# The last pipelined step of a patch-sum, attention and mixture-of-experts kernel gets an instruction order of its own

## What is computed

```python
pooled = x.reshape(B, 12, 14, 16, 14, 16).sum(axis=(3, 5))      # sums over 16x16 patches
h = einsum('bcij,ce->bije', pooled, channel_weights)            # tokens
h = h + attn(layernorm(h))      # 12 heads of 16; weights relu(1 + qk + qk^2/2), normalised by their sum
# mixture of 8 experts, the top 2 of a softmax over the router's logits
flat = layernorm(h); top_w, top_i = top_k(softmax(flat @ router_w.T), 2)
for e in range(8):
    out = out + w_e * (gelu(flat @ w1[e] + b1[e]) @ w2[e] + b2[e])
h = h + out
```

## Time and profile before

| | us |
|---|---|
| median of 3 executions | 1339.64 |
| lowest and highest | 1336.73, 1343.89 |
| the profiled execution, its own time | 1337.59 |
| its span in the trace | 1335.8 |
| PE busy in the span | 1217.7 (91%) |
| DVE, ACT, POOL busy | 903.1, 608.4, 589.5 |
| mean granted TensorE clock | 0.945 |

### The profile page before, as it was taken

How to read it: one execution, slowest core, us unless ns; L and a number is a source line. 1 busy time by engine, 2 the same in 40 slices (tenths; PEclk the granted TensorE clock), 3 DMA queues, 4 the chain that set the end, 5 groups by cost and what they waited for, 6 DMA issues and landing times.

```text
span 1335.8 us, 26425 instructions
## 1 busy us (share of the span) xinstructions
PE 1217.7 (91%) x7299; PEld 1086.3 (81%) x7299; DVE 903.1 (68%) x3022; ACT 608.4 (46%) x1159; POOL 589.5 (44%) x484
## 2 busy tenths in 40 slices
PE   5867766999999989999999999999999989999996
PEld 3756655888888878888888888888888879898996
DVE  6789887787878677878777687878764323332443
ACT  1222223454545444545454455555454534444664
POOL 0104334415545445454535545454545465433433
PEclk9986566999999999999999999999999989999998
DMA  9679887777978787878787978888735565544565
GB/s 357 231 263 333 326 279 254 237 223 242 243 243 238 231 220 239 245 242 236 245 228 226 242 239 233 249 237 250 193 99 106 170 142 109 102 96 92 118 144 113
DMA packets 126551, 284.41 MB, mean 213 GB/s; under 512 B 24820, under 2 KB 70501, under 8 KB 126501
## 3 DMA queue, kind: packets, MB, share of 16 engines
q1 hardware_dynamic: 82762, 241.95, 54.9%
q0 software_dynamic: 43104, 41.25, 18.3%
q10 hardware_dynamic: 634, 0.61, 0.2%
HBM read 228.79 MB, written 54.95 MB: 212 GB/s over the span
## 4 chain that ended last, share of the span: by engine, by line
PE 40%; DVE 17%; DMA 16%; issue 13%; POOL 11%; ACT 2%; POOLq 0%; ACTq 0%; DVEq 0%; SPq 0%
PE ps L998 13%; PE ps L967 12%; DMA result<-ys,ridx 8%; POOL rows_d L610 7%; DMA rows_d<-rows,sloti 7%; DVE red L1074 6%; POOL result L625 4%; PE ps L807 3%; PE ps L938 3%; PE ps L939 3%; DVE topi L1208 1%; DMA w1r<-L_attn_w_qkv 1%; DVE att L1192 1%; PE ps L1027 1%; PE ps L893 1%
## 5 line engine op out<-in xcount | busy, mean ns | idle before, releaser
L625 POOL DMA_INDIRECT result<-ys,ridx x210 | 329.9, 1571 | 311.0 <-issue 142.0
L998 PE MATMUL ps<-w2a,hid 128*128 x2520 | 455.6, 327 | 0.0
L998 PEld LDWEIGHTS ps<-w2a,hid 128*128 128x128 f32 x2520 | 415.8, 191 | 11.8 <-issue 0.2
L610 POOL DMA_INDIRECT rows_d<-rows,sloti x256 | 251.1, 981 | 382.8 <-DMA rows_d<-rows,sloti 158.3
L1074 DVE TENSOR_REDUCE red<-xbuf 128x21 f32<-128x672 f32 x448 | 359.0, 842 | 5.1 <-PE ps L871 2.4
L732 ACT ACTIVATE hid<-ps,b1s 128x512 f32<-128x512 f32 (+1 forms) x344 | 222.7, 654 | 235.5 <-PE ps L967 226.3
L967 PE MATMUL ps<-xh,w1h 128*128 128x512 f32 (+1 forms) x344 | 164.8, 479 | 8.9 <-DVE xl L1302 5.3
L1325 DVE TENSOR_TENSOR w1l<-w1r,w1h 128x768 fp32r<-128x768 f32 x116 | 110.4, 953 | 76.4 <-ACT w1h L744 75.7
L967 PE MATMUL ps<-xh,w1l 128*128 128x512 f32 (+1 forms) x344 | 130.5, 379 | 0.0
L967 PE MATMUL ps<-xl,w1h 128*128 128x512 f32 (+1 forms) x344 | 130.5, 379 | 0.0
L967 PE MATMUL ps<-xb,w1l 128*128 128x512 f32 (+1 forms) x344 | 130.3, 379 | 0.0
(11 more groups left out here) (160 smaller groups left out, 1569.7 us busy)
## 6 DMA issues: line engine op xcount, KB each, us to landing
xbuf<-x SPq DMA_DIRECT2D x224, 672.0 KB, 5.7
w1r<-L_ffn_w SPq DMA_DIRECT2D x118, 384.0 KB, 4.5
xr<-rows_d SPq DMA_DIRECT2D x48, 402.0 KB, 3.5
result<-h1s SPq DMA_DIRECT2D x32, 294.0 KB
w2a<-L_ffn_w SPq DMA_DIRECT2D x8, 576.0 KB, 7.8
rows_d<-rows,sloti POOLq DMA_INDIRECT x256
rows_d<-pad SPq DMA_DIRECT2D x9, 402.0 KB, 4.4
result<-ys,ridx POOLq DMA_INDIRECT x210
```

Of the source, the lines that this page charges most:

```text
L610: pool.indirect_dma_start(rows_d, bass.IndirectOffsetOnAxis(ap=sloti[:, k * NT + t:k * NT + t + 1], axis=0), rows[:, t, :], None).then_inc ...
L625: pool.indirect_dma_start(out, bass.IndirectOffsetOnAxis(ap=ridx[:, b, n:n + 1], axis=0), ys[:, b, n, :], None, compute_op=ALU.add).then_i ...
L998: last = mm(yout(g, b, n), hid[:, m % 3, cols], w, start=False, stop=m == MC - 1 and n % 2 == 1)
```

## The change

Step 15 gets lists of its own, `ORDER_END`. `ORDER` stays as it is for steps 4 to 14. No operation is added or removed; each engine carries out the same set.

```diff
+ORDER_END = [
+    """S1 M2 S2 L J N0 N1 X0 N2 S3 M3 W0 X1 N3 S4 Z0 M4 S5 B M5 W1 Z1 N4 N5 Y""".split(),
+    """M0 S6.0 M1 S6.1 M2 S6.2 N0 S6.3 N1 X0 S7.0 <I M3 S7.1 X1 N2 S8.0 S8.1 N3 W0 <F <A S8.2 Z0 S8.3 L B M4 S10 R J M5 V.0 S11 W1 Z1 V.1""".split(),
+    """S9 M0 <N4 <N5 <Y M1 V.2 V.3 <F Q0 Q1 Q2 Q3 <A M2 <I W0 N0 X0 Z0 M3 N1 N2 X1 W1 M4 I L B Z1 M5""".split(),
+    """M0 <Y <N3 <N4 <N5 <J M1 <F <A""".split(),
+]
@@ tiles_do
-                lists = TAIL_ORDER if at_end[0] else ORDER
+                lists = TAIL_ORDER if at_end[0] else ORDER if pooling else ORDER_END
```

## The result

Measured against the kernel before on the same chip, the changed kernel takes 1349.84 us against 1342.73 us (medians of 10 executions each), a ratio of 1.0044 with a 95% interval of 1.0023 to 1.0065. By the ratio that is about 5.9 us more (the medians lie 7.1 apart). The forecast was 2.5 us less, so its sign was wrong, and 1349.84 lies above the range. On two other chips the same two kernels gave 1.0021 (0.9981 to 1.0062) and 1.0089 (1.0047 to 1.0131). The profiled execution of the changed kernel took 1356.23 us, with a span of 1354.4.

The account below looks back on a forecast made before the run. The scatters' chain was taken to set PE's gap at X0 of tile 37. PE, there at 1072.5, would resume at 1074.0, 2.5 us less overall: 1335.1 us profiled, 1337.1 median, range 1332 to 1343.

Parts of the forecast that it names:

- What bounds before, and what the load waited for: X0 of tile 37: PE's gap, worth 10.2 us at most, is set by the scatters' chain; zero rows ended 8 us earlier.
- First list, 0 to 0.6 us: Step 15's first list: N3 closely follows M3 and waits for its gelu, costing 0 to 0.6 us.
- S9's wait, 4.3 us: PE at S9 from 1028.1 waits 4.3 us for `mask`, ready at 1032.4, with L on DVE ahead of S10.
- Its price in clock, 1.7 us: Behind PE's wait at S9 the clock falls, losing 1.7 us, taken from step 11's wait of 2.76 us.
- Slots and the start of the scatters, 0.7 to 0.8 us later: Slots ready at 1038.5 against 1037.74, behind V.0, W1 and Z1; scatters start at 1039.4.
- The landing waits: POOL's scatters: the first landing wait may shrink from 4.90 to 2.40 us; later groups, beside the zero rows, gain nothing.
- The stretching by DVE's subtractions: Scatters beside DVE's subtraction for w1l took 1.65 us against 0.95; fewer such overlaps save 0.4 us at most.
- PE's arrival at X0, +88.8 forecast: PE reaches X0 of tile 37 at 1066.2 + 0.3 + 4.3 + 1.7 = 1072.5.
- The zero rows, "issued at 1055.4 to 1065, so there nothing goes": Zero rows, issued at 1055.4 to 1065, lie beside the second and third scatter groups, whose landing waits then don't shrink.
- (3): Slower through ACT's queue behind V.0; zero rows land with or behind the last scatters; about 1343.5, 4 us slower; chance 0.12.
- (1): The wait only moves; a short gap at X0 lowers the clock a second time; about 1339.6; chance 0.26.
- (2): The change does what it says: no loss at S9, slots 2 us sooner; gain 8 to 10, 1330.5; chance 0.12.

Follow-up runs that it names:

- before_padwait: Kernel before, but SP waits for the zero rows' landing only ahead of tile 41's load instead of tile 38's; ratio 0.9994 to the kernel before.
- after_first_old: Changed kernel with step 15's first list as in the kernel before; ratio 1.0162 to the kernel before, on four executions.
- after: The changed kernel, first trace; 1349.84 us against 1342.73; S1 of step 15 to the first chunk behind X0 of tile 37 (the stretch) 99.8 us.
- after_L_early: Changed kernel with L and B of tile 34 moved from behind S8.3 to behind X1 in the second list; ratio 0.9979 to the kernel before.
- after_S9_later: Changed kernel with S9 behind N4 and N5 of tile 34 instead of ahead of M0 of tile 35; ratio 1.0062 to the kernel before.
- after_again: Changed kernel with nothing edited, second trace; ratio 1.0021 to the kernel before.
- after_third: Changed kernel with nothing edited, third trace; 99.6 us from S1 of step 15 to the first chunk behind X0 of tile 37.
- after_padwait: Changed kernel, but SP waits for the zero rows' landing only ahead of tile 41's load instead of tile 38's; ratio 1.0017 to the kernel before.
- flow: Changed kernel's lists rearranged: L, B, J behind X1, S9 behind N5, W1 ahead of V.0, Z1 behind S9 on DVE; ratio 0.9961 to the kernel before.
- first and third sets: Eight runs: unedited repeats of old, changed and rearranged kernels, and single edits of the changed kernel; 91.3 to 101.4 us for the stretch.
- second set: Four runs: zero-row wait moved in the kernel before, that plus L and B early, rearranged lists without and with it; stretch 94.1, 91.4, 89.4, 87.6 us.

## Why the prediction was wrong

**What bounds before, and what the load waited for: right.** before_padwait and the constant 257 us behind the stretch show it.

**First list, 0 to 0.6 us: right within what can be read** (after_first_old, under 1 us). S8.3 was forecast to end at 1025.7, +42.0. Its last product takes 0.2 us from the start in the table, so it ended at +41.9 in the traces with this list where ACT wasn't late, and at +42.7 in the trace of after.

**S9's wait, 4.3 us: right in cause and nearly in size** (3.75 us in all five traces with that order). after_L_early shows that L is 1.45 us of it. after_S9_later shows what I did not see: without it PE waits 3.33 us at N0 of tile 35, so S9's place alone was not worth 3.75 us.

**Its price in clock, 1.7 us: mis-sized.** I took the loss behind a wait of 2.76 us for a longer wait. It was 3.4 us in after and after_again, 1.7 in after_third, after_padwait and after_first_old. And I counted the gap at X0 without a fall of the clock; there was one in after, as there was before.

**Slots and the start of the scatters, 0.7 to 0.8 us later: right** (1.1 us, of which some is ACT's lateness). after_S9_later shows that they do not hang on S9's place on PE. **The landing waits: right in direction, too careful.** I let the first one shrink and kept the second at 4.9, because I had the zero rows beside it. Both were 2.3 us, for the zero rows weren't out yet. The stretching by DVE's subtractions, "0.4 us at most", was mis-sized too: 1.8 us went. The last recorded landing is at +83.1, against +84.8 to +87.7.

**PE's arrival at X0, +88.8 forecast, +92.5 measured: the first step that failed.** It was 82.5 + 0.3 + 4.3 + 1.7. It became 82.7 + 3.75 + 3.4 + 1.7 at N0 of tile 36, plus about 1 us of smaller waits in the first list. The wait at N0 of tile 36, for Y of tile 35, was in no term; it is 1.5 to 1.9 us in all five traces with those second and third lists. In flow's order it is 2.25 us in the trace where ACT was late and absent in the other two, so it seems to go with ACT's lateness; no trace of the changed lists is free of that, so this stays open.

**The zero rows, "issued at 1055.4 to 1065, so there nothing goes": the step that decided.** I computed when they are issued (+71.7) and then used it only for what they do to the scatters. Had I added their landing, 3 to 4 us behind an issue of 9.84, I would have had +71.7 + 9.8 + 4 = +85.5, level with the scatters that I had shortened; with both in one place a few more microseconds anywhere on the way would have shown as a loss. They were issued at +77.1, 5.4 us later: 1.8 us because SP came to B later than I had it, and 3.6 us for SP itself, which was slow between B and J. The chain in that trace shows it (start, us, what):

```profile
1067.46 0.70 SPq L466
...
1068.19 0.70 SPq L518
1068.89 0.70 issue
1069.59 0.00 SPq L518
```

Most of what the zero rows cost hangs on that lateness of SP, by an estimate from these numbers. From B's load to the first zero rows SP took 7.3 us in after and 4.2 in before. Had they landed 3.1 us sooner, at +88.7, the rows would have reached PE at about +93.0, and PE, there at +92.5, would have waited 0.5 us instead of 3.6. In after_again and after_third SP took 6.0 and 5.8 us for the same. What stays without it is PE's arrival: after_padwait, with the zero rows out of the way, still has a stretch of 95.8 us, 1.0 more than before's, and no gain.

The sum's "no gap" bound of 4.1 us of gain and its worst case of 0.5 us of loss both assumed the zero rows out of the way.

**Rivals.** (3), with 0.12 at 4 us slower, was the nearest: zero rows with or behind the last scatters. Its entry, PE waiting at N0 of tile 35 through ACT's queue behind V.0, is in no trace of the changed kernel, where the wait at S9 comes first and Y ends 1.0 us ahead of N0; it is in after_S9_later, with 3.33 us. (1) was right that the wait moves. (2) needed lists that put L elsewhere: flow is nearly that kernel.

## What to carry to other kernels

Before pulling a late chain forward, list all things that the stalled load waits for with their times, not only the last one. Here the second in line, some 7 us ahead, depended on PE's progress, and the change slowed just that; and a gap on an engine is also cover for everything that is late before it. And a producer's place in an order written by hand must be far enough behind what it waits for on every engine: the same pull forward lost 5 us as first written and won 5 us in flow, where L, B, J, W1, V.0, Z1, S9 and a few others stand elsewhere. Moving a producer out of the way of one wait can bring up the next, as S9's move did.

## What the runs showed of the hardware

- After the same wait of 3.75 us the clock stayed at half for 3.4 us in three traces and 6.8 us in two (mean clock over 12 us 0.86 and 0.72). After 2.30 us it stayed full in one trace and fell for 3.4 us in another; after 3.33 us it stayed full (after_S9_later), and after 1.87 us it fell (after_again). A price for one idle time, taken from one trace, can be off by a factor of two, or there can be none.
- A scatter's landing is waited for 2.3 us with the queues quiet, and 3.1 to 6.6 us with the zero rows or weights in flight, for the same scatters.
- A scatter beside DVE's subtraction of two SBUF operands is stretched: 1.20 us with half of one beside it, 1.63 with a whole one, 0.95 alone. DVE's timeline of after_S9_later:

```profile
1073.33 0.96 DVE L1331 TENSOR_TENSOR w1l<-w1r,w1h 128x768 fp32r<-128x768 f32 x1 [0.63 <-ACT w1h L750]
...
1084.85 0.95 DVE L1331 TENSOR_TENSOR w1l<-w1r,w1h 128x768 fp32r<-128x768 f32 x1
```

  and POOL's at the same times:

```profile
1073.90 1.20 POOL L616 DMA_INDIRECT rows_d<-rows,sloti  x1 [2.32 <-DMA rows_d<-rows,sloti]
...
1084.99 1.63 POOL L616 DMA_INDIRECT rows_d<-rows,sloti  x1 [3.63 <-DMA rows_d<-rows,sloti]
```

  The Trainium skill, "SBUF — State Buffer", section "Who interferes with whom", infers that tensor_tensor does not stall the writing of descriptors, and says that with both inputs in SBUF it contends with what GpSimd reads. A scatter also reads its slots from `sloti`, so the trace does not tell which of the two is stretched, and the prediction was too quick to say that it disagrees with the page; that the scatter as a whole gets longer is what it shows.
- In after SP took 0.70 us for several instructions in a row that take 0.02 elsewhere. ACT was 2 to 4 us late at one place of step 15 in after and in all traces of the first and third sets, with the new lists and with the old, and in no trace of the second set, nor in the first trace of before. The nine late traces hold 70 to 120 of the 256 landing records of step 15's scatters, the five others 253 or more, so the lateness goes with how a trace came out. Its cause stays open, and it isn't known whether executions outside these traces have it.
